# Gated window attention with layer norm, one core: five of seven input surveys and batch 0's quantised branch moved from the start into steps 0 to 8

## The chip, the cores and the metric

The kernel runs on one core of one Trainium2 chip, in one launch. The metric is device time in microseconds, the median over several executions. Engines are named as the profile names them: PE is TensorE, DVE is VectorE, ACT is ScalarE, POOL is GpSimd, SP is SyncE, which only issues transfers here.

## What is computed

Eight batches of 512 rows by 256 columns are normalised. An attention with 32 query heads, 8 key heads of width 64, rotary turning, a window of 128 to each side and a sink per head gives `s`. A linear layer on an input rounded to 4 significant bits (fp8) gives a gate `g`. The scale of that rounding comes from the largest absolute value of all eight normalised batches, so nothing of the gate of any batch can be rounded before all eight inputs have been looked at.

```python
xn = _layernorm(x)
s = attention(xn, Wq, bq, Wk, bk, Wv, bv, Wo, bo, sinks)   # softmax over |i-j| <= 128 and the sink
scale = max(max(abs(xn)) / 448, 1e-7)                       # over all eight batches
x_q = (xn / scale) rounded to float8_e4m3
g = silu(x_q @ (weight * weight_scale) + bias)
out = x + s * g
```

## The kernel before

Every engine's program is written out by hand, in order, and the engines meet at counting semaphores. The work is cut into 64 steps `it` (8 batches `n` by 8 key heads `k`), each step into four slots `q`, one for each tile of 128 rows. In slot `q` of step `it` PE makes scores of head `it`, raw score rows of head `it + 1` from which DVE takes the row maxima (`score_rows`, `maximum`), weighs the values (`weigh`) of the tile before, transposes it (`turn_o`) and projects the one before that (`out_project`). At slot 0 it also projects the queries of head `it + 2` (`queries`). These are biased by ACT (`even_out`, `odd_out`), rotated by POOL in eight instructions (`turn_even`, `turn_odd`, `first_low`, `turn_rest`, `second_low`) and brought into place by SP (`queries_in`: four transfers into `qT_full`, and later `highs_in`, one into `qT_high`). Keys go the same way (`keys_turn`, `keys_sum`, `keys_low`, `keys_high_in`, `keys_low_in`). POOL also cuts the window's corners out of the exponentials (`cut`).

Whatever doesn't belong to each step is hung into a slot: on PE by `chunk_at` (keys, values, transposed inputs), on DVE by `beside`. Each product of float32 is made of a high and a low part; a chunk of the weights is therefore loaded, copied by ACT into its high part (`chunk_high`) and subtracted into its low part (`chunk_low`, on DVE or POOL). There are eleven chunks: 0 and 1 hold keys and values, 2 and 3 the queries of heads 0 to 3, 4 and 5 those of heads 4 to 7, 6 and 8 to 10 the output weights, 7 (`FFN_CHUNK`) the gate's.

Step -1 is the start: it makes the row maxima of head 0 and projects the queries of head 1. `survey(m)` reads batch `m` (`bn_stats`, `bn_aggr`, `tensor_reduce` for the largest and the smallest of each row); there are seven, for batches 1 to 7. `widest` puts their results together, and `largest` makes the scale of them (`inv_scale`), with two small matmuls on PE and a chain of small instructions between. Before the change all seven surveys and `widest` stand ahead of step 0, and PE waits for the scale before it starts step 0:

```python
            for m in range(1, 7):
                survey(m)
            for it in range(-1, STEPS + 1):      # survey(7), widest() and largest() are in step -1
                step(it)
```

## Time and profile before

| | before |
|---|---|
| times of three executions | 1682.67, 1683.79, 1677.29 us; median 1682.67 |
| the profiled execution | 1678.36 us, of which the span of instructions is 1676.5 us |
| PE busy | 1621.8 us (97%) |
| DVE, ACT, POOL busy | 1143.2 us (68%), 989.7 us (59%), 1037.8 us (62%) |
| mean granted TensorE clock | 0.991 |

The profiled execution lies 4.3 us under the median of the three. A share of busy time is a mean over all 64 steps; the start is only a few per cent of it and has to be read by itself. A step starts on PE with the first product of `queries` (line 1176); the stretches of the windows below are cut at these places: step 0 starts at 65.80 us, step 1 at 93.79, step 2 at 126.47, step 3 at 150.13, step 4 at 173.22.

### The profile page before, as it was taken

How to read it: one execution, taken by the hardware profiler on the slowest of the kernel's cores; microseconds unless marked ns; L12 is line 12 of the kernel's file. 1: busy time of each engine (PE TensorE's matmuls, PEld its weight loads, DVE VectorE, ACT ScalarE, POOL GpSimd, SP SyncE). 2: the span in 40 equal slices, each digit the busy share in tenths (PEclk: the TensorE clock that was granted, in tenths of full speed). 3: DMA queues.
4: the chain of work that ended last, by engine and by line, in shares of the span. 5: the costliest groups of instructions: out<-in, count | busy, mean ns of one | idle time of the engine just before them, and what ended most of it. 6: DMA issues, size and time to landing. Idle time of an engine off the chain costs nothing.

```text
span 1676.5 us, 34111 instructions
## 1 busy us (share of the span) xinstructions
PE 1621.8 (97%) x11183; PEld 1457.1 (87%) x11183; DVE 1143.2 (68%) x3619; ACT 989.7 (59%) x2407; POOL 1037.8 (62%) x1016
## 2 busy tenths in 40 slices
PE   6599999999999999999999999999999999999998
PEld 4388988989898988989889898898988899898987
DVE  7756676767676667667677667676676667666664
ACT  2456665566655665656655666556655566556663
POOL 5656665676666657576576656567566666656651
PEclk9799999999999999999999999999999999999999
DMA  6644534544544543534554443643544544443550
GB/s 200 137 86 95 107 66 91 95 79 92 86 86 89 92 89 70 116 65 88 93 84 94 89 91 67 113 85 73 106 72 87 100 78 98 80 86 70 95 99 13
DMA packets 77278, 150.89 MB, mean 90 GB/s; under 512 B 12720, under 2 KB 25264, under 8 KB 73008
## 3 DMA queue, kind: packets, MB, share of 16 engines
q1 hardware_dynamic: 77104, 148.71, 45.9%
q8 instruction: 92, 1.51, 0.4%
q14 instruction: 82, 0.67, 0.2%
HBM read 18.64 MB, written 4.19 MB: 14 GB/s over the span
## 4 chain that ended last, share of the span: by engine, by line
PE 90%; DVE 3%; ACT 3%; issue 2%; DMA 1%; POOL 1%; SPq 0%; POOLq 0%; DVEq 0%
PE pv_bank L1283 29%; PE ring L1176 13%; PE ring L1241 11%; PE acc L1308 10%; PE score L1267 8%; PE score L1269 8%; PE ring L1293 4%; PE ring L1185 2%; PE ring L1166 1%; PE ring L1213 1%; ACT qT_high L711 1%; ACT prob_all L676 1%; PE acc L1192 1%; DMA gate<-in_w_all 1%; DVE junk L989 1%
## 5 line engine op out<-in xcount | busy, mean ns | idle before, releaser
L989 DVE CUSTOM_DVE_ANT_0 junk<-ring,mask,sink 128x384 bf16<-128x384 f32 (+1 forms) x1024 | 558.4, 549 | 291.8 <-PE ring L1241 273.2
L1283 PEld LDWEIGHTS pv_bank<-v,prob_all 128*128 128x128 f32 x5120 | 682.3, 191 | 30.7 <-ACT prob_all L676 11.5
L1283 PE MATMUL pv_bank<-v,prob_all 128*128 128x65 f32 x5120 | 685.4, 265 | 3.5 <-DVE o_norm L1004 1.3
L580 POOL TENSOR_SCALAR_AFFINE_SELECT prob_all<-prob_all 128x512 f32<-128x512 f32 x384 | 254.5, 677 | 450.2 <-ACT prob_all L676 450.1
L676 ACT ACTIVATE prob_all<-score 128x512 f32<-128x512 f32 x640 | 370.2, 595 | 172.8 <-PE score L1269 161.9
L1241 PE MATMUL ring<-kT_high,qT_full 128*128 128x384 f32 (+1 forms) x1024 | 371.7, 363 | 16.6 <-DVE row_max L989 7.9
L1267 PE MATMUL score<-qT_full,kT_high 128*128 128x512 f32 x640 | 263.9, 412 | 0.7
L1269 PE MATMUL score<-qT_high,kT_low 68*128 68x512 f32 x640 | 254.8, 398 | 0.0
L1241 PEld LDWEIGHTS ring<-kT_high,qT_full 128*128 128x128 f32 x1024 | 196.1, 191 | 50.4 <-DVE row_max L989 20.0
L734 ACT ACTIVATE oT_hi<-ring 128x256 fp32r<-128x256 f32 x256 | 96.5, 377 | 182.1 <-PE ring L1293 180.9
L1010 DVE TENSOR_TENSOR oT_lo<-ring,oT_hi 128x256 fp32r<-128x256 f32 x256 | 107.8, 421 | 135.9 <-ACT oT_hi L734 134.1
L711 ACT ACTIVATE qT_high<-ring,ident 4x256 fp32r<-4x256 f32 x512 | 196.0, 451 | 3.5 <-PE ring L1213 0.3
L1308 PE MATMUL acc<-wo_hi,oT_hi 128*128 128x256 f32 x512 | 155.4, 304 | 0.2 <-DVE oT_lo L1010 0.2
L540 POOL TENSOR_TENSOR q_first<-q_first,q_first_hi 128x512 f32<-128x512 f32 x64 | 83.7, 1308 | 112.6 <-ACT q_first_hi L693 112.6
L1308 PE MATMUL acc<-wo_lo,oT_hi 128*128 128x256 f32 x512 | 143.3, 280 | 0.0
L1308 PE MATMUL acc<-wo_hi,oT_lo 128*128 128x256 f32 x512 | 143.3, 280 | 0.0
L1267 PEld LDWEIGHTS score<-qT_full,kT_high 128*128 128x128 f32 x640 | 121.9, 190 | 15.6 <-ACT prob_all L676 1.8
L1176 PE MATMUL ring<-xT_hi,w_hi 128*128 128x512 f32 x320 | 130.3, 407 | 5.3 <-DVE w_lo L872 2.6
L1176 PE MATMUL ring<-xT_lo,w_hi 128*128 128x512 f32 x320 | 127.8, 399 | 0.0
L1176 PE MATMUL ring<-xT_hi,w_lo 128*128 128x512 f32 x320 | 127.2, 398 | 0.0
L1269 PEld LDWEIGHTS score<-qT_high,kT_low 68*128 68x128 f32 x640 | 121.4, 190 | 2.9
L682 ACT ACTIVATE q_even<-ring,q_bias 128x512 f32<-128x512 f32 x64 | 44.1, 689 | 129.2 <-PE ring L1176 129.2
(137 smaller groups left out, 2582.0 us busy)
## 6 DMA issues: line engine op xcount, KB each, us to landing
qT_high<-qT_full SPq DMA_DIRECT2D x64, 512.0 KB, 4.5
qT_full<-q_first SPq DMA_DIRECT2D x64, 256.0 KB, 4.2
qT_full<-q_first_hi SPq DMA_DIRECT2D x64, 256.0 KB, 5.5
qT_full<-q_second SPq DMA_DIRECT2D x64, 256.0 KB, 4.2
qT_full<-q_second_hi SPq DMA_DIRECT2D x64, 256.0 KB, 5.4
kT_high<-k_first_hi SPq DMA_DIRECT2D x128, 64.0 KB, 2.5
kT_high<-k_second_hi SPq DMA_DIRECT2D x128, 64.0 KB, 2.5
x_res<-in_x SPq DMA_DIRECT2D x10, 512.0 KB, 6.2
```

Source lines behind the costliest of these rows:

```text
L580: nc.gpsimd.affine_select(out=pr, in_=pr, compare_op=ALU.is_ge, fill=0.0, base=0, pattern=[[0, GROUP], [sign, P]], channel_multiplier=-sign) \
L676: nc.scalar.activation(prob[:, q % 2 * 3 + n, :], score[(FIRST[q] + n) % 2][:, :], ACT.Exp) \
L711: last = nc.scalar.activation(qT_high[D:D + NR, s % 2, h, pair * 2 * P:(pair + 1) * 2 * P], ring[2][0:NR, 0:2 * P], ACT.Copy, scale=ident[ ...
L734: nc.scalar.activation(oT_hi[:, q % 2, :], ring[2][:, 0:KT * P], ACT.Copy).then_inc(s_oT_hi_done, 1)
L989: nc.vector.tensor_tensor_reduce(junk[:, h % 2, 0:cols], ring[h % 2][:, 0:cols], mask[:, m0:m0 + cols], 1.0, sink[:, col:col + 1], ALU.add ...
L1010: nc.vector.tensor_tensor(oT_lo[:, q % 2, :], ring[2][:, 0:KT * P], oT_hi[:, q % 2, :].bitcast(F32), ALU.subtract).then_inc(s_oT_lo_done, 1)
L1176: last = nc.tensor.matmul(bank[:, :], w[:, k, col:col + P], xs[:, k, :], start=(n == 0), stop=(n == len(products) - 1))
L1241: nc.tensor.matmul(ring[h % 2][:, 0:cols], qT_full[:, b % 2, h, q * P:(q + 1) * P], kT_high[:, b % 3, k0 * P:k0 * P + cols], start=True, s ...
L1267: nc.tensor.matmul(score[blk % 2][:, :], kT_high[:, c % 3, k * P:(k + 1) * P], qT_full[:, c % 2, :, q * P:(q + 1) * P], start=True, stop=F ...
L1269: nc.tensor.matmul(score[blk % 2][:, :], kT_low[0:D + NR, c % 3, k * P:(k + 1) * P], qT_high[0:D + NR, c % 2, :, q * P:(q + 1) * P], start ...
L1283: last = nc.tensor.matmul(pv[:, h, :], prob[:, q % 2 * 3 + n, h * P:(h + 1) * P], v[:, slot, k, :], start=(n == 0), stop=(n == len(BLOCKS[ ...
L1308: last = nc.tensor.matmul(acc[q // 2][:, (q % 2) * M:(q % 2 + 1) * M], left[:, q % 2, k * P:(k + 1) * P], right[:, col:col + M], start=fre ...
```

## The change

Surveys 1 and 2 stay at the start. Surveys 3 to 7 are split into three parts and hang in `beside` in steps 0, 1 and 2; `widest` stands in slot 3 of step 2, `largest` in slot 0 of step 3. Batch 0's rounding (`exponents`, `quantise`, `quantised`) goes from step 0 to steps 3 and 4, its transposition on PE (`turn_xq`) from slot 2 of step 0 to slots 1 and 2 of step 4, its gate matmuls (`ffn`) from step 1 to steps 5 and 6, and the rest of the gate to steps 5 to 8; batch 1's normalisation goes from steps 1 to 4 into steps 4 and 5. In SP's program of step 0 the transfer of `x_in` goes and those of the missing surveys and chunks stand before and behind the queries'. The chunks are handled in the order `CHUNK_ORDER`; chunks 2 and 3 are loaded ahead of the constants, and their low parts are made by POOL, not DVE. The projections of queries and values at the start have PSUM banks of their own, so none waits for another's reader. The idle PE work at the start (`turn_over`) goes from 32 + 12 matmuls to 16 and one behind each row product of step -1. POOL still rotates the queries of heads 0 and 1.

```diff
+CHUNK_ORDER = (0, 1, 2, 3, 6, 4, 7, 5, 8, 9, 10)
+def ffn_at(n, k, q):
+    slots = ((5, 0), (6, 0)) if n == 0 else ((1, 0), (1, 2))
+    return slots.index((k, q)) if 0 <= n < BATCH and (k, q) in slots else None
...
+    if n == 0 and (k, q) in ((4, 1), (4, 2)):
+        return ("xq", 0, q - 1)
```

SP's program at the start:

```diff
             load_chunk(0)
             load_chunk(1)
+            load_chunk(2)
+            load_chunk(3)
+            for dst, src in turns:
+                sp.dma_start(dst, src).then_inc(s_turn_in, 16)
+            load_first_x(1)
             for dst, src in consts:
                 sp.dma_start(dst, src).then_inc(s_const_in, 16)
-            load_chunk(2)
-            load_chunk(3)
-            load_first_x(1)
```

SP's program in `step(it)`:

```diff
+                if it == 0:
+                    sp.wait_ge(s_late_lo_done, low_count(4))
+                    load_chunk(5)
+                    sp.wait_ge(s_row_done, 3)
+                    load_first_x(5)
+                if it == 1:
+                    sp.wait_ge(s_row_done, 5)
+                    load_first_x(7)
                 if real(a):
                     queries_in(a, False)
                     queries_in(a, True)
```

POOL's program, at the start and in `step(it)`:

```diff
             rstd_of(0)
+            chunk_low(2)
+            chunk_low(3)
             keys_sum(0)
...
-            rows_rstd(1, 4)
+            chunk_low(6)
             turn_even(1)
...
+                    if it == 0 and q == 0:
+                        chunk_low(4)
+                    if it == 2 and q == 3:
+                        rows_rstd(5, 7)
                     if real(it):
                         cut(it, q)
```

DVE's program at the start:

```diff
             chunk_low(0)
+            chunk_low(1)
             x_low(0, 0)
             x_low(0, 1)
-            chunk_low(1)
-            chunk_low(2)
-            chunk_low(3)
```

DVE's `beside(it, n, k, q)`:

```diff
+                if n == 0:
+                    if it == 0:
+                        if q == 0:
+                            survey_spread(3)
+                            survey_max(3)
+                        elif q == 1:
+                            survey_min(3)
+                        elif q == 2:
+                            survey_spread(4)
+                        else:
+                            survey_max(4)
+                            survey_min(4)
```

PE's program at the start:

```diff
+            project_values(0, pv_bank)
+            project_values(1, acc[0])
+            project_values(2, ring[2])
             for it in range(-1, STEPS + 1):
                 step(it)
```

How the rows of two engines stand now: each row is one instruction of the program, with its line, its kind, what it writes and reads, and how often it repeats. First DVE from the end of the keys' turning in the start; `x_ends` is the surveys' result, `junk` a row maximum. Before:

```order
L966 SCALAR_TENSOR_TENSOR k_second_hi<-ring,k_bias,cos 128x512
L842 BN_STATS stats<-x_res 128x6 x4
L843 TENSOR_REDUCE x_ends<-x_res 128x4
L844 TENSOR_REDUCE x_ends<-x_res 128x4
L849 BN_AGGR x_moments<-stats 128x2 x4
```

This group of four rows of a survey stands six times in a row before the values (`v`) and the first `junk`. After the change:

```order
L1034 SCALAR_TENSOR_TENSOR k_second_hi<-ring,k_bias,cos 128x512
L897 BN_STATS stats<-x_res 128x6 x4
L901 BN_AGGR x_moments<-stats 128x2 x4
L907 TENSOR_REDUCE x_ends<-x_res 128x4
L912 TENSOR_REDUCE x_ends<-x_res 128x4
L1042 TENSOR_TENSOR v<-pv_bank,v_bias 128x7x64
```

Four surveys are gone from this place, and the values stand behind the first one. Next POOL at the start, from the first reciprocal root on (`rstd`) to the first rotated queries. Before:

```order
L499 TENSOR_TENSOR rstd<-var_eps,minus_half_all 128x4
L551 TENSOR_TENSOR k_first<-k_first,k_first_hi 128x512
L553 TENSOR_TENSOR k_second<-k_second,k_second_hi 128x512
L521 TENSOR_TENSOR q_first<-q_even,cos 128x512
```

After:

```order
L528 TENSOR_TENSOR rstd<-rstd,minus_half_all 128x4
L543 TENSOR_TENSOR w_lo<-prob_all,w_hi 128x1024
L543 TENSOR_TENSOR w_lo<-gate,w_hi 128x1024
L580 TENSOR_TENSOR k_first<-k_first,k_first_hi 128x512
L582 TENSOR_TENSOR k_second<-k_second,k_second_hi 128x512
L550 TENSOR_TENSOR q_first<-q_even,cos 128x512
```

Two low parts of weights have come ahead of the keys. Last POOL in slots 2 and 3 of step 2, where the queries of head 4 are rotated (`cut` is AFFINE_SELECT). Before:

```order
L536 TENSOR_TENSOR q_second<-q_second,q_odd 128x512
L580 AFFINE_SELECT prob_all<-prob_all 128x512
L545 TENSOR_TENSOR q_second<-q_second,q_second_hi 128x512
```

After:

```order
L565 TENSOR_TENSOR q_second<-q_second,q_odd 128x512
L534 TENSOR_TENSOR x_rstd<-x_moments,eps_all 128x12
L536 TENSOR_TENSOR x_rstd<-x_rstd,minus_half_all 128x12
L609 AFFINE_SELECT prob_all<-prob_all 128x512
L574 TENSOR_TENSOR q_second<-q_second,q_second_hi 128x512
```

The two instructions of `rows_rstd(5, 7)` now stand ahead of that slot's cut and of the last part of the queries.

## Rows read from the trace of the kernel before

**Rows 1.** Head of the page.

```profile
span 1676.5 us, 34111 instructions
```

**Rows 2.** Windows: stretch, length, busy us of each engine, granted clock, DMA share, GB/s.

```profile
43.00:65.80 22.80, 9.33 (x25) 4.85 (x23) 19.94 (x56) 7.97 (x16) 20.60 (x14) 0.63 0.93 204
65.80:93.79 27.99, 23.65 (x141) 19.79 (x141) 17.98 (x50) 16.73 (x38) 16.82 (x15) 0.93 0.25 52
93.79:126.47 32.68, 29.80 (x194) 26.67 (x193) 19.12 (x64) 15.42 (x38) 17.10 (x18) 0.95 0.47 99
126.47:150.13 23.66, 23.29 (x166) 21.03 (x165) 14.30 (x51) 15.36 (x38) 18.89 (x19) 1.00 0.40 74
150.13:173.22 23.09, 23.05 (x167) 20.95 (x166) 16.31 (x52) 15.56 (x39) 14.24 (x15) 1.00 0.57 110
```

**Rows 3.** Timeline of PE: start, length, instruction; in brackets the wait before it.

```profile
44.47 0.28 PE L1241 MATMUL ring<-kT_high,qT_full 128*128 128x256 f32 x1
64.20 0.37 PE L1318 MATMUL ring<-ident,amax 128*1 128x128 f32 x1 [4.65 <-DVE amax L865]
65.81 0.80 PE L1176 MATMUL ring<-xT_hi,w_hi 128*128 128x512 f32 x1
74.59 0.28 PE L1241 MATMUL ring<-kT_high,qT_full 128*128 128x256 f32 x1
103.06 0.44 PE L1293 MATMUL ring<-ident,o_norm 128*128 128x128 f32 x2 [2.81 <-DVE gate L909]
```

**Rows 4.** Timeline of POOL at the start.

```profile
22.34 1.28 POOL L551 TENSOR_TENSOR k_first<-k_first,k_first_hi 128x512 f32<-128x512 f32 x1 [14.12 <-DVE k_second_hi L966]
...
44.21 1.27 POOL L521 TENSOR_TENSOR q_first<-q_even,cos 128x512 f32<-128x512 f32 x1 [2.66 <-DMA qT_full<-q_second_hi]
```

**Rows 5.** Timeline of SP's queue: when a transfer is issued.

```profile
33.89 0.62 SPq L389 DMA_DIRECT2D qT_full<-q_first  x1
...
53.12 0.58 SPq L389 DMA_DIRECT2D qT_full<-q_first  x1
...
64.79 0.50 SPq L397 DMA_DIRECT2D qT_high<-qT_full  x1
```

**Rows 6.** Timeline of DVE: a low part of weights, two surveys' first rows.

```profile
18.40 1.23 DVE L872 TENSOR_TENSOR w_lo<-gate,w_hi 128x1024 fp32r<-128x1024 f32 x1
...
22.18 1.39 DVE L842 BATCH_NORM_STATS2 stats<-x_res 128x6 f32<-128x256 f32 x4
...
26.21 1.41 DVE L842 BATCH_NORM_STATS2 stats<-prob_all 128x6 f32<-128x256 f32 x4
```

**Rows 7.** Timelines of DVE and of POOL over the same stretch.

```profile
76.42 2.75 DVE L891 TENSOR_TENSOR x_in<-x_in,ffn_e 128x512 f32<-128x512 f32 x1
...
76.24 2.38 POOL L514 TENSOR_TENSOR wo_lo<-x_res,wo_hi 128x1024 fp32r<-128x1024 f32 x1 [4.94 <-ACT wo_hi L644]
```

**Rows 8.** Timeline of DVE in slot 0 of a later batch's step 7.

```profile
451.03 1.12 DVE L898 TENSOR_TENSOR xq<-x_in,ffn_e 128x512 bf16<-128x512 f32 x1
...
453.30 0.48 DVE L989 CUSTOM_DVE_ANT_0 junk<-ring,mask,sink 128x256 bf16<-128x256 f32 x1
```

**Rows 9.** Timelines at steps 2 and 3: POOL, SP, PE; POOL's root at the start.

```profile
56.87 2.28 POOL L507 TENSOR_TENSOR x_rstd<-x_var,minus_half_all 128x12 f32<-128x12 f32 x1
...
149.69 1.29 POOL L545 TENSOR_TENSOR q_second<-q_second,q_second_hi 128x512 f32<-128x512 f32 x1
...
157.07 0.51 SPq L397 DMA_DIRECT2D qT_high<-qT_full  x1
...
157.48 0.28 PE L1241 MATMUL ring<-kT_high,qT_full 128*128 128x256 f32 x1
```

**Rows 10.** Timeline of PE: a gate's eight matmuls to the next product; the rounded input's transposes.

```profile
112.28 0.28 PE L1166 MATMUL ring<-ffn_hi,xqT 128*128 128x256 f32 x1
...
113.24 0.40 PE L1176 MATMUL ring<-xT_hi,w_hi 128*128 128x512 f32 x1
...
83.39 0.62 PE L1153 MATMUL ring<-ident_b,xq 128*128 128x128 bf16 x8
```

More of the change, by code:

```diff
@@ L627, in _ @@
             second_low(1)
-            chunk_low(4)
-            rows_rstd(5, 7)
-            for n in range(5, FFN_CHUNK + 1):
-                chunk_low(n)
             for it in range(STEPS + 1):
@@ L669, in ffn_exp @@
                 act.wait_ge(s_ffn_clamped, n * 2 + j + 1)
-                nc.scalar.activation(ffn_e[:, :, :], ffn_e[:, :, :], ACT.Exp, scale=-1.0) \
+                e = ffn_e if n else ffn_e_first
+                nc.scalar.activation(e[:, :, :], e[:, :, :], ACT.Exp, scale=-1.0) \
                     .then_inc(s_ffn_exp, 1)
@@ new lines, in beside @@
+                if n == 0:
[10 more added lines that the diff above has]
+                            survey_min(4)
+                    elif it == 1:
+                        if q == 0:
+                            survey_spread(5)
+                            survey_max(5)
+                        elif q == 1:
+                            survey_min(5)
+                            survey_spread(6)
+                        elif q == 2:
+                            survey_max(6)
+                        else:
+                            survey_min(6)
+                    elif it == 2:
+                        if q == 0:
+                            survey_spread(7)
+                            survey_max(7)
+                        elif q == 1:
+                            survey_min(7)
+                            widest_first()
+                        elif q == 3:
+                            widest()
+                    elif (k, q) == (3, 0):
+                        largest()
+                    elif (k, q) == (3, 2):
+                        dve.wait_ge(s_late_lo_done, low_count(FFN_CHUNK))
+                        exponents(0, 0)
+                        quantise(0, 0)
+                    elif (k, q) == (3, 3):
+                        quantised(0, 0)
+                        exponents(0, 1)
+                    elif (k, q) == (4, 0):
+                        quantise(0, 1)
+                        quantised(0, 1)
+                    elif (k, q) == (4, 3):
+                        dve.wait_ge(s_x_got, 32)
+                        statistics(x_in, range(TILES))
+                        moments_of(1)
+                    elif (k, q) == (5, 1):
+                        normalise(1, x_in, range(TILES))
+                    if (k, q) == (5, 1):
+                        ffn_clamp(0, 0)
+                    elif (k, q) == (5, 2):
+                        ffn_one_more(0, 0)
+                    elif (k, q) == (5, 3):
+                        ffn_invert(0, 0, 0)
+                    elif (k, q) in ((6, 0), (6, 1), (6, 2)):
+                        ffn_invert(0, 0, q + 1)
+                    elif (k, q) == (6, 3):
+                        ffn_gate(0, 0)
+                        ffn_clamp(0, 1)
+                    elif (k, q) == (7, 0):
+                        ffn_one_more(0, 1)
+                    elif k == 7:
+                        ffn_invert(0, 1, q - 1)
@@ L1085, in step @@
                     order = heads_at(it, q)
-                    if (it, q) == (-1, 0):
-                        for t in range(TILES - 1):
-                            values(0, t)
                     first = (k, q) == (KV - 1, 1) and it >= 0 and other is not None
@@ L1126, in _ @@
             chunk_low(0)
+            chunk_low(1)
             x_low(0, 0)
             x_low(0, 1)
-            chunk_low(1)
-            chunk_low(2)
-            chunk_low(3)
-            dve.wait_ge(s_const_in, 16 * len(consts))
+            dve.wait_ge(s_turn_in, 16 * len(turns))
             keys_turn(0, 0)
             keys_turn(0, 1)
-            for m in range(1, 7):
-                survey(m)
+            survey_spread(1)
+            survey_max(1)
+            survey_min(1)
+            dve.wait_ge(s_const_in, 16 * len(consts))
+            for t in range(TILES - 1):
+                values(0, t)
+            for m in range(2, 3):
+                survey_spread(m)
+                survey_max(m)
+                survey_min(m)
             for it in range(-1, STEPS + 1):
@@ L1192, in turn_over, with warm @@
                     nc.tensor.matmul(acc[1][:, :], ident_r[:, :], xT_hi[:, 0, :], start=True, stop=True)
+            def warm(count):
+                for _ in range(count):
+                    nc.tensor.matmul(acc[1][:, 0:P], ident_r[:, :], ident_r[:, :], start=True, stop=True)
             def queries(a, odd):
                 if a == 0:
-                    pe.wait_ge(s_w_lo_done, FIRST_CHUNKS)
-                    pe.wait_ge(s_k_turned, 4 if odd else 2)
+                    pe.wait_ge(s_late_lo_done, low_count(3))
                 elif odd:
```

282 lines of the change are left out of this document (159 added, 123 removed).

## The prediction

> **What bounds the kernel now.** The windows come first, cut at the step starts. In step 3 PE is busy for 23.05 of 23.09 us at the full clock [rows 2]: from there on PE sets the pace, with gaps too small to win anything, and a step of its own work is 23.1 us. The change touches nothing there. The start is different. From 43.00 to 65.80 PE does 9.3 us of work in 22.8 at a granted clock of 0.63, while DVE is busy for 19.9 us and POOL for 20.6; step 0 takes 28.0 us, step 1 32.7, step 2 23.7 [rows 2]. Time can be won ahead of step 2 only.
>
> The timelines tell what is waited for. PE has its first row product at 44.47, when the first queries have landed. It then waits for the surveys and the scale: 4.65 us for `amax` at the end, and step 0 starts at 65.81 [rows 3]. A second chain runs beside it: POOL turns the keys from 22.34, then the queries of head 0, and those of head 1 from 44.21, when the transfers of the first have landed [rows 4]. SP issues the first transfer of head 0's queries at 33.89 and of head 1's at 53.12; the four of head 1 have all landed at 64.79, where the transfer that waits for them is issued [rows 5]. PE's first row product of head 1, in slot 1 of step 0, is only at 74.59 [rows 3], 9.8 us later. So the scale is the last wait, and the queries of head 1 are the next one, some 10 us shorter. That product is the best mark to cost the change with.
>
> **The change, part by part.** The sum is made against the profiled execution, 1678.4 us for a span of 1676.5 [rows 1]; that is 4.3 us below the median of the three times.
>
> *1. The mark in step 0.* The scale no longer stands ahead of step 0, so the chain of the queries ends last. How much earlier does that start? Before, DVE's turning of the keys began behind its fourth low part of weights, at 18.40 + 1.23 [rows 6]. Two of these four go to POOL, worth up to 2.5 us. Against that, chunk 1's stands ahead of `x_low` now, for which PE waits, so 1.2 us come back. POOL's own two (2.4 us each, the price of `wo_lo` [rows 7]) lie in its wait of 14.1 us before 22.34 [rows 4]. The bounds are 0 and 2.5 us; I take 1.2.
>
> One row speaks for the lower end. A DVE instruction with two inputs in SBUF took 2.75 us while POOL's `wo_lo` of 2.38 us ran, and ended when that was over [rows 7]. POOL's low part of chunk 2 can run just when DVE wants chunk 1's. The Trainium skill, SBUF — State Buffer, section Who interferes with whom, says that a Vector instruction with two SBUF inputs and a GpSimd instruction that reads SBUF exclude each other for their whole length; the trace agrees (2.75 us). By that rule the gain of the chain would be 0 and the whole sum 12.3 us instead of 13.5; were there no such lock, it would be 2.5 and the sum 14.8.
>
> The eight rotations of each head stay on POOL, and head 1's still wait for head 0's transfers, which took 44.21 - 33.89 = 10.3 us [rows 4, 5]. Head 1's took 64.79 - 53.12 = 11.7 us in a stretch in which the DMA engines were 93% busy [rows 2], with weights among it; most of these are gone from this place, so I take 10.3 again. Landing is then at 64.8 - 1.2 - 1.4 = 62.2, and the mark at 62.4: **-12.2 us**. PE can be there: it begins its rows at 43.0, twelve row maxima at 0.8 us are 10 us, and slot 0 took 74.59 - 65.81 = 8.8 us [rows 3], together 61.8.
>
> *2. Slots 1 to 3 of step 0* took 93.79 - 74.59 = 19.2 us [rows 2, 3]. Of that 2.1 us were the lock above (2.75 for an operation of 0.7), and 0.6 the rounded input's transposes on PE, which go [rows 7, 10]. What is left is 16.5 us. In its place DVE gets surveys 3 and 4. One is 26.21 - 22.18 = 4.0 us [rows 6]. DVE had 14.3 us of work in step 2 [rows 2]; with 8.1 us of surveys and 0.8 for values it has about 23 us in a step of 24. The sum fits, the single slot is tighter: slot 0 gets 2.9 us at once. The nearest that the trace shows is 453.30 - 451.03 = 2.3 us between two row maxima, which costs PE nothing [rows 8]. For the 0.6 us more in slots 0, and a lower clock behind the wait at the mark, I add 1.5: 18.0 us, **-1.2**. Bounds 16.5 and 21.
>
> *3. Step 1* took 32.7 us. In it are 2.8 us of waiting for `gate`, behind a late transfer of batch 1 [rows 3], about 2 us for a clock that fell to half after that (0.95 in the mean of 32.7 us is 1.6) and the gate's matmuls, 113.24 - 112.28 = 0.96 us, twice [rows 2, 10]. All three go. What is left is 26.0 us of PE. DVE has 14.3 + 8.1 + 2.8 for keys = 25.2. With 1 us for collisions: 27.0, **-5.7**. Bounds 26 and 31.
>
> *4. Steps 2 to 3.* `rows_rstd(5, 7)` takes 2.28 us [rows 9], some 2.5 with the small addition ahead of it, on POOL, ahead of slot 3's cut and of the last part of head 4's queries, which ended at 149.69 + 1.29. Those queries landed at 157.07, and PE's product that needs them is at 157.48 [rows 9]: 0.4 us to spare. POOL is the late one here, since it was busy for 18.9 of the 23.7 us [rows 2]. So 2.1 of the 2.5 us come through; DVE also stands in `widest` for the roots, ahead of its share for PE, in the same stretch. **+2.3** to that product. Bounds 0 and 4.
>
> *5. Batch 0's branch, later.* Gate and transposes, 1.9 + 0.6 = 2.5 us of PE [rows 10], come back in steps 4 to 6, which are full. The scale's small chain in slot 0 of step 3 costs 0.5 to 1. **+3.3.** ACT's share of it and the late weights have room (ACT 15.6 of 23.1 us [rows 2]) and I cost them at nothing; POOL's late low parts come at slot ends where it waits for exponentials. If this cover were gone in one step, it would cost 2.4 us. On SP the load of survey 5 stands ahead of the queries of head 2 and waits for survey 3's end in slot 1; these queries are ready only in slot 2, so nothing is queued behind it.
>
> Sum: -12.2 - 1.2 - 5.7 + 2.3 + 3.3 = **-13.5 us**. The profiled execution would be 1664.9 us, the median 1669.2. I say 1667, between the two.
>
> **The rivals.**
> *More is won.* The chain starts 2.5 us earlier and the mark is at 61.1, steps 0 and 1 run at PE's own work (16.5 and 26.0), and DVE's wait and POOL's root lie over each other: -13.5 - 2.7 - 6.7 + 0 + 2.5 = -20.4, so 1658 us. For it: PE hid 2.3 us of DVE between two maxima. Against it: three slots with 2.9 us, and the margin of 0.4 us.
>
> *DVE becomes the bound of steps 0 to 2.* No gain in the chain (mark at 63.6, -11.0), slots 1 to 3 21 us (+1.8), step 1 31 us (-1.7), +4 and +3.5 behind: -3.4, so 1675 us on the profiled execution's level, which can't be told from no change. For it: 23 of 24 and 25 of 26 us leave DVE no room for waiting on PE. Against it: I counted its 14.3 us in full, though 2 us of those are extras of step 2. It would be so too if the surveys weren't the last wait in the start; the 4.65 us say they are.
>
> *PE's clock stays at half; slower.* From 43 to 65.8, with waits of several us, the granted clock was 0.63 [rows 2]. Work that is 23.1 us a step at 2.4 GHz is some 43 at 1.2. If short waits on DVE kept the clock low through one and a half steps, 30 us would be added and the time is 1695; it gets slower by more than 0.5% from about 22 us on, a whole step at half. Against it: in step 0 the clock was 0.93 in the mean though PE had come out of a long wait, so it rises when PE has work. The Trainium skill, TensorE: Matmul & The Clock Gate, section HAM oscillation, describes matmul streams that fall back to the lower clock at each wait for data; here only the stretch before 65.8 looks like it.
>
> **How the numbers follow.** 0.5% is 8.4 us, about what a measurement of this kernel can tell from no change. Chances: the forecast (9 to 17 us won) 0.54, more won 0.18, DVE the bound 0.21, clock 0.07. Of the forecast and its neighbour 0.72 lie beyond 0.5%; within it 0.20; slower 0.08. The range goes from the higher gain to the level of the DVE case on the median: 1658 to 1677.
>
> **What would show it.** Right: PE's first row product of head 1 near 62, released by the transfers of `qT_full`; step 1 starting near 80, step 2 near 107 and step 4 near 157; `amax` between 128 and 134, with DVE waiting for `x_rstd`. Wrong: that product waits for DVE; waits of PE on `row_max` add up to over 5 us in steps 0 to 2; a granted clock under 0.9 in them; or steps 4 to 8 longer by more than their 2.5 us.

## The result, and the profile after

The changed kernel takes 1675.48 us (median of 20 executions, 1671.64 to 1681.14) against 1682.78 us (20 executions, 1677.19 to 1686.17): a ratio of 0.9962, with a 95% interval of 0.9952 to 0.9972. The medians lie 7.3 us apart where I had said 13.5 on either level. The profiled execution took 1675.05 us, only 3.3 us less than that of before, which had been 4.3 us under its own median. So 4.0 of the 7.3 us are not in the two profiles, and no run shows where they come from. The median lies inside the range that I gave, 1658 to 1677, but that is luck: the upper end was the time of the DVE rival, whose mechanism didn't come.

The head of the page of the changed kernel, which answers to [rows 1]:

```profile
span 1673.3 us, 34109 instructions
```

PE's timeline of the changed kernel: the first row product of head 0, the start of step 0, the last wait ahead of the mark, the first row product of head 1 (the mark), the transposition of `amax`, and the row product of head 4. They answer to [rows 3, 9]:

```profile
42.09 0.36 PE L1381 MATMUL ring<-kT_high,qT_full 128*128 128x256 f32 x1 [3.23 <-issue]
...
53.90 0.79 PE L1310 MATMUL ring<-xT_hi,w_hi 128*128 128x512 f32 x1 [0.45 <-DVE row_max L1057]
...
61.58 0.39 PE L1381 MATMUL ring<-kT_high,qT_full 128*128 128x256 f32 x1 [1.14 <-DVE row_max L1057]
...
62.27 0.28 PE L1381 MATMUL ring<-kT_high,qT_full 128*128 128x256 f32 x1
...
137.43 0.27 PE L1457 MATMUL ring<-ident_r,amax 128*1 128x128 f32 x1
...
142.95 0.36 PE L1381 MATMUL ring<-kT_high,qT_full 128*128 128x256 f32 x1 [0.76 <-issue]
```

The mark moved from 74.59 to 62.27 us; I had said 62.4. But PE did not wait for the queries' transfers there: they had landed at 61.49, and the last wait ahead of the mark is the one of 1.14 us for a row maximum. The two chains behind it, on POOL and on SP's queue, answer to [rows 4, 5]:

```profile
20.02 1.29 POOL L580 TENSOR_TENSOR k_first<-k_first,k_first_hi 128x512 f32<-128x512 f32 x1 [3.71 <-DVE k_second_hi L1034]
...
42.16 1.28 POOL L550 TENSOR_TENSOR q_first<-q_even,cos 128x512 f32<-128x512 f32 x1 [3.53 <-DMA qT_full<-q_second_hi]
```

```profile
31.50 0.62 SPq L409 DMA_DIRECT2D qT_full<-q_first  x1
...
51.11 0.58 SPq L409 DMA_DIRECT2D qT_full<-q_first  x1
...
61.49 0.51 SPq L417 DMA_DIRECT2D qT_high<-qT_full  x1
```

Windows of the changed kernel, cut at the starts of steps 0 to 9, with the columns of [rows 2]:

```profile
53.90:80.57 26.67, 24.06 (x132) 19.96 (x133) 17.57 (x61) 13.80 (x35) 15.62 (x16) 0.89 0.64 121
80.57:108.53 27.96, 26.71 (x179) 23.43 (x177) 24.50 (x75) 16.12 (x38) 20.63 (x19) 1.00 0.58 129
108.53:133.60 25.07, 23.48 (x166) 21.09 (x165) 17.38 (x58) 15.26 (x39) 19.43 (x19) 1.00 0.54 119
133.60:158.89 25.29, 24.36 (x170) 21.30 (x168) 17.81 (x60) 16.82 (x39) 18.55 (x18) 1.00 0.44 80
158.89:184.63 25.74, 23.76 (x174) 21.27 (x173) 19.03 (x57) 15.73 (x39) 17.02 (x16) 1.00 0.50 98
184.63:214.30 29.67, 26.88 (x188) 23.99 (x187) 22.95 (x67) 16.05 (x39) 15.53 (x17) 1.00 0.38 75
214.30:241.07 26.77, 25.53 (x180) 22.98 (x179) 19.78 (x57) 16.40 (x39) 17.19 (x17) 1.00 0.33 58
241.07:270.65 29.58, 28.14 (x184) 24.29 (x183) 24.61 (x67) 15.21 (x37) 16.66 (x16) 1.00 0.59 102
270.65:295.29 24.64, 24.64 (x181) 22.48 (x180) 17.70 (x55) 15.61 (x38) 14.48 (x14) 1.00 0.50 91
```

The same steps 3 to 8 before, from its windows (the first of them is in [rows 2]):

```profile
173.22:196.30 23.08, 23.02 (x167) 20.95 (x166) 15.30 (x53) 14.96 (x38) 16.40 (x16) 1.00 0.46 86
196.30:222.01 25.71, 25.64 (x181) 23.16 (x179) 19.31 (x58) 15.65 (x39) 14.30 (x15) 1.00 0.53 107
222.01:247.88 25.87, 24.73 (x172) 22.00 (x171) 18.28 (x54) 16.40 (x39) 17.54 (x17) 1.00 0.33 60
247.88:275.49 27.61, 27.36 (x185) 24.26 (x183) 19.25 (x61) 14.69 (x36) 17.12 (x16) 1.00 0.51 83
275.49:300.05 24.56, 24.56 (x181) 22.40 (x179) 16.28 (x53) 15.59 (x38) 13.54 (x14) 1.00 0.52 101
```

Set the two tables beside each other. At the start of step 2 the changed kernel is 126.47 - 108.53 = 17.9 us ahead, at step 3 16.5, at step 4 14.3, at step 9 only 300.05 - 295.29 = 4.8. Steps 3 to 7 take 137.05 us instead of 125.36. PE is busy for 4.9 us more in them, which holds the work that was moved; the other 6.8 us are gaps. One gap is long. PE's timeline in slot 2 of step 5:

```profile
201.30 1.06 PE L1280 MATMUL ring<-ident_r,x_in 128*128 128x128 f32 x8 [2.69 <-DVE oT_lo L1078]
```

What DVE and POOL did ahead of it, two timelines over the same stretch:

```profile
196.15 4.33 DVE L883 TENSOR_SCALAR x_in<-x_in,moments,rstd 128x256 f32<-128x256 f32 x4
200.41 0.41 DVE L986 TENSOR_SCALAR x_late<-gate 128x512 f32<-128x512 f32 x1
200.74 0.41 DVE L1078 TENSOR_TENSOR oT_lo<-ring,oT_hi 128x256 fp32r<-128x256 f32 x1
```

```profile
195.06 1.27 POOL L550 TENSOR_TENSOR q_first<-q_even,cos 128x512 f32<-128x512 f32 x1
196.28 1.42 POOL L551 TENSOR_TENSOR q_second<-q_even,sin 128x512 f32<-128x512 f32 x1
197.66 1.33 POOL L556 TENSOR_TENSOR q_second_hi<-q_odd,sin 128x512 f32<-128x512 f32 x1
199.07 1.26 POOL L558 TENSOR_TENSOR q_first<-q_first,q_second_hi 128x512 f32<-128x512 f32 x1
```

Batch 1's normalisation, four small instructions of DVE, lasts as long as POOL's four rotations and ends with them (200.4 and 200.3 us). `oT_lo` is queued behind it, and PE waits for that. This gave the theory, **the lock**: in its new slots the branch's DVE work lies beside POOL's instructions with two inputs (here the rotations) and is held up by them. The trace of before has such a row as well, which isn't among the ones that I costed with: in its step 6, at 241.29, the second instruction of `exponents` takes 1.39 us beside POOL's rotation, and 0.43 at 252.13. The first rival of this theory, **volume**: DVE simply has more to do in steps that were full (22.95 against 19.31 us in step 5), wherever it stands.

### The profile page after: what moved, and what is told of

The parts are those of the page before. It is cut to its first block, busy times and chain, and to the rows that moved or that the text cites. A ratio compares the mean times of both kernels' runs of the same rounds, so it can differ in the third digit from the quotient of the medians.

```text
span 1673.3 us, 34109 instructions
## 1 busy us (share of the span) xinstructions
PE 1623.7 (97%) x11181; PEld 1457.8 (87%) x11181; DVE 1144.0 (68%) x3617; ACT 989.0 (59%) x2407; POOL 1042.1 (62%) x1017
## 4 chain that ended last, share of the span: by engine, by line
PE 88%; DVE 5%; issue 3%; ACT 2%; POOL 1%; DMA 1%; SPq 0%; POOLq 0%; DVEq 0%
PE pv_bank L1423 28%; PE ring L1310 13%; PE ring L1381 11%; PE acc L1448 10%; PE score L1407 8%; PE score L1409 8%; PE ring L1433 4%; PE ring L1319 2%; PE ring L1300 1%; DVE junk L1057 1%; PE ring L1353 1%; ACT qT_high L753 1%; ACT prob_all L718 1%; DMA qT_full<-q_second_hi 1%; PE ring L1280 0%
## 5 line engine op out<-in xcount | busy, mean ns | idle before, releaser
L753 ACT ACTIVATE qT_high<-ring,ident_r 4x256 fp32r<-4x256 f32 x512 | 196.0, 451 | 3.9 <-PE ring L1353 0.7
```

The costliest lines, as they stand in the source:

```text
L753: last = nc.scalar.activation(qT_high[D:D + NR, s % 2, h, pair * 2 * P:(pair + 1) * 2 * P], ring[2][0:NR, 0:2 * P], ACT.Copy, scale=ident[ ...
```

## The experiments

All times are medians. Each kernel was timed against the kernel before on the same chip; the ratio is to that. Where the text names profiles, it is one execution of each.

**1 and 2: the normalisation out of the rotations, and as much other work put back.**

```diff
-                    elif (k, q) == (5, 1):
+                    elif (k, q) == (5, 0):
                         normalise(1, x_in, range(TILES))
```

> Edit: batch 1's normalisation (four TENSOR_SCALAR on DVE) goes from slot 1 of step 5 to slot 0, where POOL has no two-input instruction; nothing else changes. Lock theory (DVE's instructions on batch 0's branch are stretched because they lie beside POOL's): the four take 1.4 us together instead of 4.33, PE's wait of 2.7 us for oT_lo in step 5 goes, step 5 takes 26.7 to 27.3 us instead of 29.7, and the median is 2.4 to 3 us below the changed kernel's 1675.5: about 1672.8. Volume theory (DVE simply has more work in these steps, it matters little where): the same work is done in the same step, step 5 stays above 29 us and the time within 0.5 us of 1675.5.

In the second, beside that edit:

```diff
                     if (k, q) == (5, 1):
+                        dve.wait_ge(s_xn_done, 2)
+                        nc.vector.tensor_reduce(x_ends[:, 0:TILES], x_in[:, :, :], AX.X, ALU.max)
                         ffn_clamp(0, 0)
```

> Edit: the same as the first, and in slot 1 of step 5 DVE gets a reduction of 4 x 256 columns instead (its result is used by nobody), an instruction of 1.2 us that was never stretched beside POOL in steps 0 to 2. Lock theory: the reduction takes 1.2 us, step 5 is at most 0.6 us longer than in the first, the time about 1673. Volume theory: putting as much work back into the slot brings the wait of 2.7 us back, step 5 is above 29 us and the time 1675.5.

Measured: 1670.71 us (0.9930, 0.9912 to 0.9949) and 1670.52 us (0.9927, 0.9907 to 0.9947). DVE's timeline of the first and of the second:

```profile
184.63 1.70 DVE L883 TENSOR_SCALAR x_in<-x_in,moments,rstd 128x256 f32<-128x256 f32 x4
```

```profile
196.45 1.22 DVE L1153 TENSOR_REDUCE x_ends<-x_in 128x4 f32<-128x1024 f32 x1
```

Step 5 took 27.37 and 27.38 us. The wait is gone, and about as much work in the old slot (1.22 us) doesn't bring it back. Volume falls as the cause of this wait. But the median fell by 4.8 us and the step by 2.3 only; the next runs point to a reason.

**3 and 4: exponents and root to other slots.** The first edit moves two DVE instructions, the second POOL's root.

```diff
                         quantised(0, 0)
-                        exponents(0, 1)
                     elif (k, q) == (4, 0):
+                        exponents(0, 1)
                         quantise(0, 1)
```

> Edit: exponents(0, 1), two TENSOR_SCALAR of DVE, go from slot 3 of step 3 to slot 0 of step 4, ahead of the addition that follows them. Lock theory: they take 0.42 and 0.43 us instead of 1.32 and 2.52, the wait of 0.9 us of PE for o_norm at 163.8 goes and a part of the gaps too small for the list; steps 3 and 4 together get 1 to 2 us shorter (51.0 to about 49.5), time about 1674. Volume theory: slot 0 of step 4 now has 2.6 us of extra work in a row, steps 3 and 4 together stay at 51.0 or get longer, time 1675.5 or more.

```diff
-                    if it == 2 and q == 3:
-                        rows_rstd(5, 7)
...
                         keys_sum(quad)
+                    if it == 2 and q == 0:
+                        rows_rstd(5, 7)
```

> Edit: POOL's rows_rstd(5, 7), the root over 12 rows' values of 2.3 us, goes from the front of slot 3 of step 2 to slot 0 of step 2, between keys_sum and keys_low, where POOL was idle for 3.2 us. If the late root and the late queries behind it are what made steps 2 and 3 longer than before (25.1 and 25.3 us against 23.7 and 23.1), DVE's wait of 2.1 us for x_rstd goes, head 4's queries land 2 us earlier, steps 2 and 3 together get 2 to 2.5 us shorter, time about 1673.3. If DVE's and PE's small instructions of the scale's chain are the cost, they stay as long as they are and the time stays within 0.5 us of 1675.5.

Measured: 1677.41 us (0.9971, 0.9958 to 0.9984) and 1677.11 us (0.9970, 0.9954 to 0.9986): no gain, where I had expected about 1674 and 1673.3. The traces do show one: step 4 takes 24.99 us instead of 25.74 in the one, step 3 takes 23.90 instead of 25.29 in the other (24.8 in most of the other profiles without the edit, so 0.9 us are the root's). Step 2 stays at 25.1: the root wasn't its cost. And step 5 takes 34.16 and 34.15 us in these two profiles. Windows of the run with the moved exponents, from the start of step 5 to the end of the wait, and from there to step 6:

```profile
183.54:200.20 16.66, 13.97 (x95) 12.23 (x94) 12.07 (x38) 7.70 (x19) 8.44 (x10) 0.99 0.43 91
200.20:217.70 17.50, 17.42 (x94) 16.31 (x94) 11.18 (x30) 8.53 (x21) 7.07 (x7) 0.71 0.25 42
```

The same stretch of the changed kernel:

```profile
201.30:214.30 13.00, 12.91 (x93) 11.75 (x94) 10.90 (x30) 8.33 (x21) 7.09 (x7) 1.00 0.32 56
```

The same instructions of PE take 17.5 us at a mean granted clock of 0.71 and 13.0 at 1.00. PE went into the wait at 2.4 GHz and came out of it at 1.2 in one execution and not in the other: 4.5 us.

**5: hold DVE as long, without the lock.**

```diff
                     if (k, q) == (5, 1):
+                        dve.wait_ge(s_xn_done, 2)
+                        for i, part in enumerate((M, M, M, M // 2)):
+                            nc.vector.tensor_reduce(x_ends[:, TILES * i:TILES * i + TILES], x_in[:, :, 0:part], AX.X, ALU.max)
```

> Edit: the normalisation in slot 0 of step 5 as in the first run, and in slot 1 DVE gets four reductions (three of 4 x 256 columns, one of 4 x 128; nobody uses the results), about 4.2 us, so that it is held as long as the normalisation beside POOL held it, but by instructions that are not stretched. If what counts is the time for which DVE is held there, PE waits 2.5 to 2.7 us for oT_lo again, TensorE's granted clock falls to half behind that wait in some executions (0.71 over 17.5 us, 4.5 us more, in two of the profiles so far), and the times spread from about 1671 to 1680, median 1674 to 1677. If the stretching itself or POOL's side of it is what costs, the wait is short and the median stays within 1 us of the first run's 1670.7.

Measured: 1675.04 us (0.9970, 0.9953 to 0.9987), executions from 1674.1 to 1683.9. DVE's timeline and PE's:

```profile
194.03 4.06 DVE L1154 TENSOR_REDUCE x_ends<-x_in 128x4 f32<-128x1024 f32 x4
```

```profile
198.90 1.07 PE L1283 MATMUL ring<-ident_r,x_in 128*128 128x128 f32 x8 [2.42 <-DVE oT_lo L1078]
```

Step 5 is back at 29.49 us and the median is that of the changed kernel. What costs is the time for which DVE is held in that slot. The spread came out narrower than I had said: eight of the nine executions lie between 1674.1 and 1676.5, and in the profile the half clock fell in step 6 (29.52 us), not behind this wait. The lock matters because it makes 4.3 us out of 1.4.

**6: an eighth of the columns.**

```diff
+                    part = buf[:, t, 0:32] if i == 1 else buf[:, t, :]
-                    last = nc.vector.tensor_scalar(buf[:, t, :], buf[:, t, :], ...
+                    last = nc.vector.tensor_scalar(part, part, ...
...
+                if m == 0:
+                    val, big = val[:, :, 0:32], big[:, :, 0:32]
```

> Edit to the changed kernel: the instructions of DVE for batch 0's branch (exponents, quantise, the one added, the reciprocals, the gate's product) and for batch 1's normalisation work on an eighth of their columns; the rounded input of batch 0 is zero. So the outputs of batches 0 and 1 are not the reference's; PE's, ACT's and POOL's work is unchanged. It bounds what DVE's share of the branch costs. If it is all of the excess over my forecast in steps 3 to 7, these take 25 + 25 + 27 + 26 + 28 = 131 us instead of 137, with no half clock in step 5: about 1668. If PE's own part and the order on ACT are the cost, steps 3, 4, 6, 7 stay within 0.3 us of 25.3, 25.7, 26.8, 29.6, and only step 5's wait goes: 1670.5.

Measured: 1674.94 us (0.9961, 0.9947 to 0.9975), which is the changed kernel's time; neither of my numbers. DVE's timeline of slots 2 and 3 of step 3, and of slot 1 of step 5:

```profile
151.84 0.19 DVE L949 TENSOR_SCALAR ffn_e<-x_in 128x64 uint32<-128x64 uint32 x1
152.07 0.20 DVE L952 TENSOR_SCALAR ffn_e<-ffn_e 128x64 f32<-128x64 f32 x1
...
158.10 1.09 DVE L949 TENSOR_SCALAR ffn_e<-x_in 128x64 uint32<-128x64 uint32 x1
159.23 2.32 DVE L952 TENSOR_SCALAR ffn_e<-ffn_e 128x64 f32<-128x64 f32 x1
...
194.90 2.92 DVE L884 TENSOR_SCALAR x_in<-x_in,moments,rstd 128x32 f32<-128x32 f32 x4
```

This is the clearest evidence for the lock. The same instruction of 64 columns takes 0.20 us in one slot and 2.32 in the next, beside one instruction of POOL, the low part of a chunk of the weights (`wo_lo`, 2.39 us from 159.10). So it isn't the rotations alone. An eighth of the work is not an eighth of the time; PE still waits for 2.35 us in step 5, and the clock was at half behind it (0.88 in the mean of 14.4 us), and once more in step 6, which took 29.58 us. That hides a gain: steps 3, 4 and 7 took 24.69, 24.87 and 27.97 us, 3.1 less than in the profile of the changed kernel, steps 5 and 6 (30.69 and 29.58) 3.8 more.

**7: lighter surveys**, on top of the first run's edit.

```diff
+            def few(m):
+                return first_x(m)[:, :, 0:16] if m > 2 else first_x(m)
```

> Edit to the first run's kernel: the largest and smallest of surveys 3 to 7 are taken over 16 of each row's 256 columns, so DVE has about 1.1 us less ten times in steps 0 to 2 (the scale, and with it every output, can differ from the reference's). If DVE's volume lengthens steps 0 to 2 (rival: DVE bounds them), they get 3 to 6 us shorter together (78.7 to about 75); by my forecast, in which the surveys lie beside PE's work and only collisions cost, 1 to 2 us: step 1 27.0 and step 2 24.5, time about 1669.

Measured: 1668.29 us (0.9922, 0.9907 to 0.9938), 2.4 us below the first run. Step 1 took 26.15 instead of 27.98 us, step 2 23.66 instead of 25.07, which is step 2 of before. So the surveys' reductions cost 3.2 us in steps 1 and 2, more than I had put there, and less than the rival "DVE becomes the bound". They took 1.2 us each wherever they stood, so here it is DVE's volume and not the lock. Slots 1 to 3 of step 0 stayed at 18.3 us with the lighter surveys.

**8: four edits together.** The ones of 1, 3 and 4, and in the second half of batch 0's gate:

```diff
-                    elif (k, q) == (6, 3):
+                    elif (k, q) == (7, 0):
                         ffn_gate(0, 0)
                         ffn_clamp(0, 1)
-                    elif (k, q) == (7, 0):
+                    elif (k, q) == (7, 1):
                         ffn_one_more(0, 1)
```

> Edits together: normalisation in slot 0 of step 5, exponents(0, 1) in slot 0 of step 4, the root in slot 0 of step 2, and the first half's gate product and the second half's clamp of batch 0 from slot 3 of step 6 to slot 0 of step 7 (the rest of the second half a slot later, ACT's exponential with the clamp). If stretched instructions are the cost, step 3 is 23.9, step 4 25.0, step 5 27.4, step 6 at most 26.3 and step 7 at most 29.2 us, and the time about 1668, the lowest so far. If the last edit only moves work onto another full slot, steps 6 and 7 together stay at 56.4 or more, and the time is 1669 to 1670.

Measured: 1672.3 us (0.9944, 0.9929 to 0.9960), not 1668, though the steps came out as said: 23.94, 24.98, 27.34, 26.78 (not 26.3) and 28.97 us. In this profile the start took it back: step 1 began at 81.18 us, in that of the first run at 78.24, though the programs are the same up to there. No profile says how that is spread over the executions (1670.8 to 1673.2).

**9 to 12: idle work in the start, ACT's order, and which of the edits count.**

```diff
+                    if it == -1 and q == 0:
+                        turn_over(16)
                     if q == 0 and real(it + 2):
                         queries(it + 2, 0)
...
                     if it == -1 and q == 0:
-                        turn_over(16)
+                        turn_over(28)
+                    if it == -1 and q == 3:
+                        turn_over(8)
```

> Edit to the combined kernel: more idle work of PE in the start, 16 matmuls ahead of head 1's first product (PE waits 4.8 us for q_even there), 28 in place of 16 before the first row products, 8 ahead of the transposition of neg_parts. In this stretch the granted clock was 0.50 to 1.00 in pieces of 4 us, and two runs with the same program up to step 2 had step 1 at 78.2 and 81.2 us. If the clock behind these waits is what differs, it stays above 0.9 from 30 to 66 us, step 1 begins at 77.5 to 78.5, the runs spread less, and the median is 2 to 3 us below the combined kernel's: about 1669.5. If the chain of the queries on POOL and DVE sets the start whatever PE's clock, or the fillers delay PE's own products, step 1 begins at 80 or later and the time is the same.

```diff
+                    if (it, q) == (4, 1):
+                        xq_turned(0, 0)
                     if q == 1 and real(it):
                         max_rows(it, 1)
```

> Edit to the combined kernel: in slot 1 of step 4 ACT copies the transposed rounded input (xqT) ahead of the four copies of row maxima (1.5 us), not behind them. PE waits 1.03 us for that copy in each trace so far, a row product behind it. If nothing else is late there, step 4 takes 24.0 instead of 25.0 us, time 1671.3. If PE then waits for the row maxima instead, step 4 stays at 24.7 or more.

> Edits: those of the combined kernel, the idle work and ACT's order together. Sum of the parts: 1672.3 - 2.5 - 1.0 = about 1669, and below both kernels by more than 0.3%. If the parts are not independent (the start's gain depends on where the half clock falls), 1670 to 1672.

> Edits: the normalisation in slot 0 of step 5, the idle work and ACT's order, without the three others (exponents in slot 0 of step 4, early root, gate product and clamp in slot 0 of step 7). By the traces these three shorten steps 3, 4 and 7 by 0.9, 0.8 and 0.6 us, so this should be 2.3 us above the run with all edits; if the shorter steps are given back elsewhere, the two are equal.

Measured: 1672.6 (0.9945, 0.9928 to 0.9961), 1670.82 (0.9941, 0.9926 to 0.9955), 1671.38 (0.9944, 0.9927 to 0.9960) and 1671.29 us (0.9941, 0.9926 to 0.9956): all four the same as the eighth. PE's wait for `xqT` went, but step 4 took 24.72 us instead of 24.98; I had said 24.0, or 24.7 and more if PE then waited for something else, and it does: three waits of 0.3 to 0.4 us, the longest for a row maximum.

With the idle work step 1 began at 80.5 to 80.8 us in the three profiles, no earlier. The traces show why. It did hold the clock (from 28 to 40 us 1.00 in the ninth run, 0.72 in the changed kernel), and PE came to the mark sooner, but there it now waits 0.8 us until the queries' transfers have landed (62.20 in the ninth run, the mark at 62.24). That is the case in which the chain on POOL and SP sets the start. (The changed kernel has a little more idle work in its start than the section on the change says: ten and four short matmuls, `warm`, ahead of and behind the transposes of `x`.)

The twelfth run was to tell which edits count. Its profile is 2.3 us longer than the eleventh's up to step 9 (292.48 and 290.23), as I had said of the three edits, and its median is the same. The mean granted clocks of its six executions are 0.996 to 0.998, those of the eleventh's 0.992 to 0.996: what the edits give seems to be lost to the clock. Windows of step 6 told more. The ninth run, then the eighth, from the start of step 6 to a wait in its slot 2, and from there to step 7:

```profile
209.83:231.79 21.96, 21.07 (x143) 18.74 (x142) 15.75 (x45) 13.08 (x29) 12.62 (x13) 1.00 0.27 42
231.79:239.37 7.58, 7.26 (x37) 7.04 (x38) 5.47 (x16) 3.35 (x11) 6.77 (x6) 0.61 0.78 132
```

```profile
210.51:232.47 21.96, 21.02 (x143) 18.69 (x141) 15.79 (x45) 13.05 (x29) 12.62 (x13) 1.00 0.27 41
232.47:237.29 4.82, 4.49 (x37) 4.27 (x38) 4.18 (x13) 3.35 (x11) 4.58 (x5) 1.00 0.61 131
```

The same work takes 7.58 us at a clock of 0.61 and 4.82 at 1.00. The wait between the two windows, in PE's timeline of the eighth run, and what DVE was held by:

```profile
232.47 0.28 PE L1354 MATMUL ring<-ident_r,neg_parts 128*4 128x128 f32 x2 [0.86 <-DVE oT_lo L1078]
```

```profile
230.69 1.40 DVE L949 TENSOR_SCALAR ffn_e<-ffn_e 128x512 f32<-128x512 f32 x1
```

It is the lock again, `exponents(1, 0)` beside POOL's rotation, in a place that the change didn't touch: PE waits 0.76 us for the same tile in the trace of before, ahead of 243.07.

**13 to 15: this wait taken away.**

```diff
-                    if (k, q) == (6, 2):
+                    if (k, q) == ((6, 2) if n else (6, 0)):
                         exponents(m, 0)
...
-                    if (k, q) == (6, 0) and 1 <= n + 1 < BATCH:
+                    if (k, q) == ((6, 0) if n else (5, 3)) and 1 <= n + 1 < BATCH:
                         scale_x(n + 1)
```

> Edit to the run with ACT's other order (and the four edits of the combined kernel): batch 1's scaling on ACT goes from slot 0 of step 6 to slot 3 of step 5, and exponents(1, 0) on DVE from slot 2 of step 6, where it took 1.40 us for 0.43 beside POOL's rotation, to slot 0. If the waits of 0.8 and 0.3 us behind it are what lets the granted clock fall to half in step 6 (four profiles of eleven so far), step 6 takes 25.6 to 26.0 us in every profile, no stretch behind step 1 is at half, and the median is 2 to 3 us below 1670.8: about 1668.3. If the half clock has another cause, it comes back somewhere in steps 5 to 8, and the median stays above 1670.

> Edit to the changed kernel as it is: only the shift of batch 1's scaling and exponents(1, 0) out of slot 2 of step 6. Step 5 keeps its wait of 2.7 us and its chance of a half clock. Step 6 gets 0.9 us shorter, and about 2.7 us more where the half clock fell there: median 1673.5 to 1674.5, 1 to 2 us below the changed kernel's. If the half clock moves to the next wait instead, the median stays at 1675.

> All edits: those of the first of this call and the idle work of PE in the start. With both later places cleared, the idle work shows what it gives by itself: step 1 begins at 80.5 to 80.8 in two profiles with it and at 80.8 to 81.2 in two without, so I expect at most 0.5 us, 1667.8; if it also makes the clock steadier there, 1667.

Measured: 1666.68 (0.9892, 0.9868 to 0.9917), 1674.99 (0.9939, 0.9915 to 0.9962) and 1668.14 us (0.9900, 0.9878 to 0.9922). The thirteenth beats both kernels: its median is 8.8 us below that of the changed kernel and 16.9 below that of the kernel before as timed beside it (1683.54). Its five executions lie between 1666.2 and 1667.3. Its windows of steps 3 to 7:

```profile
131.68:155.57 23.89, 23.86 (x170) 21.36 (x168) 15.80 (x56) 16.78 (x39) 16.16 (x16) 1.00 0.43 84
155.57:180.29 24.72, 23.74 (x174) 21.42 (x173) 16.89 (x56) 15.75 (x39) 16.82 (x16) 1.00 0.51 102
180.29:207.63 27.34, 26.77 (x189) 24.12 (x187) 21.24 (x67) 17.21 (x40) 15.57 (x17) 1.00 0.44 82
207.63:233.31 25.68, 25.36 (x180) 23.13 (x179) 18.39 (x56) 15.45 (x38) 15.93 (x16) 1.00 0.29 54
233.31:262.53 29.22, 27.75 (x185) 24.42 (x184) 22.71 (x66) 15.08 (x37) 17.93 (x17) 1.00 0.64 108
```

The fourteenth shows that one cleared place is not enough: step 6 takes 25.69 us, but its executions go from 1670.4 to 1678.2, with step 5's wait still there (29.64 us in the profile, which is the fastest of them). Those up to 1671.3 have a mean granted clock of 0.995, those from 1676 on one of 0.990 or 0.991. Its median isn't in the range that I gave, 1673.5 to 1674.5, but at that of the other case, 1675. The fifteenth shows that the idle work isn't worth anything: 1.5 us more than without. There I was wrong. (Step 1 at 80.2 instead of 78.6 us in the profiles says little: without the idle work it began anywhere from 78.2 to 81.2.)

Counted over all profiles, the half clock fell in step 5 in three of the six that have its wait of 2.3 to 2.7 us (runs 3, 4 and 6), and in none of the ten that don't; in step 6 in four of the thirteen that have its waits (runs 5, 6, 9 and 10; I had counted four of eleven), and in none of the three that don't.

## Why the prediction was wrong, by its steps

*1. The mark in step 0: right in its number, and partly by luck.* -12.3 us for -12.2. I had the transfers as the last to come, at 62.2, and PE there from 61.8 on. They landed at 61.49, and PE, held up for 1.14 us by a row maximum, was the later one, at 62.27. Inside it the keys' chain began 2.3 us earlier (20.02), where I took 1.2, and head 0's transfers took 42.16 - 31.50 = 10.7, head 1's 61.49 - 51.11 = 10.4 us for 10.3 each.

*2. Slots 1 to 3 of step 0: right.* 80.57 - 62.27 = 18.3 us for 18.0. The 1.5 us that I had added for fuller slots 0 and a lower clock are the clock's alone: in the profiles of runs 1, 4, 5, 13 and 14, with the clock back at 1.00 from 60 us on, it is 16.7 us, and the lighter surveys of run 7 changed nothing.

*3. Step 1: right in its mechanism, 1 us short.* 27.96 for 27.0. With the surveys light it was 26.15, so DVE's share costs 1.8 us and not 1.

*4. Steps 2 to 3: mis-sized and half misplaced.* From the start of step 2 to head 4's row product it is 34.4 us, for 33.3 (31.0 before). The root is worth 0.9 us, in step 3 (run 4); another part is the survey in step 2, 1.4 us by run 7, which I hadn't counted. That makes 2.3 of the 3.4 us; the other 1.1 I haven't followed up. The timelines agree with the rest of the mechanism. POOL and DVE in the changed kernel:

```profile
132.16 2.28 POOL L536 TENSOR_TENSOR x_rstd<-x_rstd,minus_half_all 128x12 f32<-128x12 f32 x1
```

```profile
134.48 0.63 DVE L926 TENSOR_TENSOR x_ends<-x_ends,x_moments 128x56 f32<-128x56 f32 x1 [2.11 <-POOL x_rstd L536]
```

At that product the forecast was 16.8 us ahead of before, the kernel 157.48 - 142.95 = 14.5.

*5. Batch 0's branch, later: this step failed.* I had it at +3.3 us, as PE's own work, with the rest at nothing. From head 4's row product to the start of step 9 it is 152.3 us instead of 142.6: +9.8 in the profiled execution, with no half clock in it. Where the clock falls in step 5 it is 4.5 us more (run 3). What was wrong is the sentence that costs the other engines at nothing. I asked what ACT, POOL and the weights had room for, and never where DVE's share of the branch lands. It was the term for which my own [rows 7] had the price: a DVE instruction beside POOL's lasts as long as POOL's. I used them for the mark, and not here. At the mark the lock went the other way: beside DVE's two low parts POOL's took 3.63 us instead of 2.36 (from 10.35), and that lay in POOL's wait.

The runs divide the 9.8 us. Run 13 takes 147.4 us for the same stretch (139.72 to 287.15), so 4.9 go with its edits: 2.3 in step 5, with the normalisation alone, 1.0 in step 4, 1.1 in step 6 (whose wait the kernel before has too) and 0.4 in step 7. 4.9 are left for my 3.3. In whole steps 3 to 7 run 13 is 5.5 us over the kernel before, 3.7 of PE's busy time (127.5 against 123.8 us) and 1.8 of gaps that I haven't followed up.

Added up, the terms are -12.3 - 0.9 - 4.7 + 3.4 + 9.8, and 1.5 us more come behind step 9: -3.2 us for -13.5. Of the 10.3 us between them 6.5 are the branch's, 1.1 those of steps 2 and 3, 1.0 step 1's, 0.2 step 0's, and 1.5 have no term.

Of the signs that I had named, step 1 starting near 80 (80.57) came, and so did DVE's wait for `x_rstd`; steps 2 and 4 started 1.5 and 1.9 us late, and `amax` at 137.43 and not by 134. Of those against me, waits on `row_max` stayed at 2.0 us in steps 0 to 2, the clock of step 0 was 0.89, just under 0.9, and steps 4 to 8 were 9.6 us longer and not 2.5, which is the failed step.

*The half clock.* I had it as a rival for steps 0 to 2, and there it was in step 0 alone (0.89, then 1.00), worth 1.6 us by the profiles that differ in it. It came where I didn't look. (The price was low too: I put 43 us on a step of 23.1 at half the clock, and twice 23.1 is 46.) The rival's chance was on the wrong place, its mechanism fits what came: behind a wait of 2.7 us 4.5 us more in some executions, behind one of 0.8 and one of 0.3 us 2.8 more. The Trainium skill, TensorE: Matmul & The Clock Gate, section HAM oscillation, describes it for a stream that waits for data again and again; here the half clock followed single waits in a stream that is otherwise 97% busy, in some executions.

*The rival "DVE becomes the bound"* has the measured time, 1675 us, and not for its reason: it put 31 us on step 1 and no gain on the chain, which gained 3.3 us (61.49 for 64.79). The forecast's other end, 1658, assumed that nothing collides.

Open: from step 10 on the profile of the changed kernel is 1.5 us longer than that of before (1350.0 and 1348.5 us), and so are the other profiles with the new order, by 0.4 to 3.8 us. Where the kernel before loses 4.3 us between its profiled execution and its median is open as well. And that the half clock follows from the wait is shown by its absence from the profiles of the edits that take the wait away, and by the narrow spread of runs 13 and 15 (ten executions, 1666.2 to 1669.0), not by its working; step 6's three profiles without it are few.

## What to carry to other kernels

When work of VectorE is moved, cost it by the slot into which it goes: list what GpSimd runs there, and take the end of GpSimd's instructions, not the length of VectorE's own. Look for slots in which GpSimd has little to do with two inputs; here they were the first of steps 5 and 6, and the normalisation took 1.70 us there instead of 4.33, without a wait of TensorE. (It doesn't hold for the first slot of each step: GpSimd sums keys in that of step 2.) And if a kernel's executions are scattered over 10 us, look for short waits of TensorE behind which the granted clock differs from one profile to the next: each can cost more than its length, and the gain of an edit elsewhere may not show before they are gone.

## What the hardware showed that I had not expected

- The lock takes in VectorE instructions with one tensor in SBUF, not only those with two: a TENSOR_SCALAR on 128x64 elements took 0.20 us alone and 2.32 beside one of GpSimd (2.39 us, `wo_lo`). The Trainium skill, SBUF — State Buffer, section Who interferes with whom, has this case too (an instruction in a mode that uses both ports), and the trace agrees; I had read the section for two inputs alone. TENSOR_REDUCE over 1024 elements took 1.2 us in each place, beside GpSimd or not.
- Four small ones in a row don't get through together: 2.92 us for 4 x 32 columns, 4.33 for 4 x 256, beside GpSimd; 1.70 in a slot in which it had none but a small one. Often one gets in (0.41 us for the first of the four) and the next ones wait.
- A granted clock of one half followed waits of 0.8 to 2.7 us in some executions of a program and not in others (step 6 with its waits: 26.8 us in nine profiles, 28.9 to 29.6 in four; step 5 with its wait: half in three profiles of six).
